# Convolution output and QKV stage joined in one pipeline over batches, Q and K in tiles of 128 rows, attention stacks of batch 0 loaded within it

## The reference, cut to what matters

```
x = x + _L0_conv_ref(_gn(x), ...)          # scan; at its end: layer norm over channels, * ln_weight + ln_bias, gelu
t = _to_tokens(x)
t = t + _L1_attn_ref(_ln_t(t), ...)        # ln, q k v = z @ qkv_w.T + qkv_b, scores + relative bias, softmax, proj
t = t + _L1_ffn_ref(_ln_t(t), ...)
```

## Time and profile before

| what | us |
|---|---|
| median of 3 runs (lowest, highest) | 2886.11 (2885.58, 2888.05) |
| profiled execution, own time | 2886.54 |
| its span | 2884.5 |
| scan, to its last sum | 1398.8 |
| convolution output | 48.7 |
| QKV stage | 131.5 |
| attention up to the first score | 15.2 |

### The profile page before, as it was taken

The page is one execution under the profiler, slowest core; times in us unless marked ns, Lnnn a source line. Parts: engine busy times, 40 slices in busy tenths (PEclk is TensorE's granted clock), DMA queues, the critical chain, the costliest instruction groups (busy, mean ns, idle before and its releaser), DMA issues. The chain is left out here.

```text
span 2884.5 us, 32999 instructions
## 1 busy us (share of the span) xinstructions
PE 2266.9 (79%) x8803; PEld 801.2 (28%) x8803; DVE 2114.8 (73%) x2874; ACT 1339.7 (46%) x1866; POOL 1406.6 (49%) x714
## 2 busy tenths in 40 slices
PE   3676666666666666656576799999999879999999
PEld 1111111111111111111133123322333236766766
DVE  4999999999999999999555788787878652221212
ACT  3445444544454444445455167676767532212121
POOL 3999999999999999999721100000000020000000
PEclk9666757767776766777688599999999979999999
DMA  4544544454455444544314411321312340000000
GB/s 120 173 149 159 179 157 150 161 182 157 140 167 175 164 141 162 173 161 147 117 51 104 54 24 25 42 29 24 46 24 31 61 107 6 6 6 6 6 6 11
DMA packets 97109, 274.03 MB, mean 95 GB/s; under 512 B 16958, under 2 KB 22657, under 8 KB 96897
## 3 DMA queue, kind: packets, MB, share of 16 engines
q1 hardware_dynamic: 92858, 271.89, 33.4%
q10 hardware_dynamic: 4078, 0.19, 0.1%
HBM read 226.55 MB, written 41.22 MB: 93 GB/s over the span
## 5 line engine op out<-in xcount | busy, mean ns | idle before, releaser
L607 POOL TENSOR_TENSOR hs<-hs,c_rep 128x1024 f32<-128x1024 f32 x384 | 897.4, 2355 | 81.1 <-DVE hs L703 51.5
L451 PE MATMUL psU<-b_stack,b_sel 96*128 96x512 bf16 x640 | 310.9, 498 | 451.1 <-DVE hs L703 448.7
L1595 DVE TENSOR_REDUCE mx<-ps 128x1 f32<-128x512 f32 x864 | 539.4, 683 | 115.4 <-PE ps L1434 110.3
L1570 ACT ACTIVATE P<-ps 128x512 f32<-128x512 f32 x768 | 417.7, 599 | 247.1 <-PE ps L1446 223.0
L653 DVE TENSOR_TENSOR psU<-psU,dtu_rep 128x512 f32<-128x512 f32 x640 | 431.3, 679 | 26.8 <-DMA dtu_rep<-dt_rows 10.9
L419 PE MATMUL psY<-hs,state_sel 128*32 128x512 f32 x1572 | 425.9, 904 | 13.8 <-POOL hs L607 8.9
L547 ACT ACTIVATE decay<-dt_rep,a_neg 128x1024 f32<-128x1024 f32 x320 | 360.5, 1140 | 158.4 <-DVE hs L703 134.6
L703 DVE TENSOR_TENSOR_SCAN hs<-decay,hs,psU 128x512 f32<-128x512 f32 x320 | 408.0, 1275 | 2.3
L703 DVE TENSOR_TENSOR_SCAN hs<-decay,psU 128x512 f32<-128x512 f32 x320 | 388.2, 1213 | 0.0
L1434 PE MATMUL ps<-ks,qs 96*128 96x512 bf16 x864 | 344.7, 403 | 34.4 <-DMA ks<-qk_parts 23.8
L451 PEld LDWEIGHTS psU<-b_stack,b_sel 96*128 96x128 bf16 x640 | 62.7, 100 | 975.8 <-DVE hs L703 876.2
(11 more groups left out here) (226 smaller groups left out, 2377.5 us busy)
## 6 DMA issues: line engine op xcount, KB each, us to landing
c_rep<-bc_rows SPq DMA_DIRECT2D x132, 512.0 KB, 4.9
dt_rep<-dt_rows SPq DMA_DIRECT2D x99, 512.0 KB, 4.7
dtu_rep<-dt_rows SPq DMA_DIRECT2D x99, 512.0 KB, 6.3
b_rep<-bc_rows SPq DMA_DIRECT2D x33, 512.0 KB, 6.1
dt_rows<-dt SPq DMA_DIRECT2D x33, 384.0 KB, 3.3
dt_rows<-soft SPq DMA_DIRECT2D x33, 384.0 KB, 3.4
qs<-qk_parts SPq DMA_DIRECT2D x90, 128.0 KB, 6.6
ks<-qk_parts SPq DMA_DIRECT2D x90, 128.0 KB, 7.2
```

The costliest lines, as they stand in the source:

```text
L451: pe.matmul(psU[:, q % UR, :], s.b_sel[:, r, nq, :], b_stack[:, p, CH * pos:CH * pos + CH], start=True, stop=True).then_inc(b_spread, 1)
L607: pool.tensor_tensor(h, h, c_rep[:, nq, :], ALU.mult).then_inc(hc_ready, 1)
L1570: nc.scalar.activation(P[:, kt % 2, head, :], ps2[:, bank, :], ACT.Exp).then_inc(exp_done, 1)
L1595: v.reduce_max(mx[:, slot, u:u + 1], ps1[:, (slot * MAXES + u) % R, :], AX.X).then_inc(max_done, 1)
```

## The change

`conv_out` and `qkv` become one function, `mid`. It runs 24 groups, six a batch: a group is one chunk of 512 tokens and 128 of the 384 rows of Q and K. Both norms are cut into steps, kind 0 for the one ahead of the GELU and kind 1 for the one ahead of Q, K and V. `norm_steps` places them in the groups: kind 0 two batches ahead in groups 0 to 3, kind 1 one batch ahead in groups 3 to 5. GELU of the next batch is run in group 0 (group 1 in batch 0), with a table load before and behind it; x is added in the group after. All norms share a ring of four working buffers in the order of FIRST. The low part is made by POOL (`low_part`), no longer by DVE. The projection's weights and the corner table are prepared before the first group and in group 2, and their copies made in groups 6 and 7. SP loads the stacks of batch 0 in groups 8 to 16, four DMAs each, behind the store of the group. The table's double copy in DRAM is made in `prepare`. V holds 16 columns a head instead of 32, and attention clears and sets its padded copy itself. `layer_norm` stays for the experts' norm.

The core of the diff:

```diff
+Q_PARTS, K_PARTS = [0, 0, 1, 1, 0, 2], [0, 1, 0, 1, 2, 0]
...
+                sp.dma_start(s.ext[0:19, :], w.table).then_inc(tab_ext, 16)
+                sp.dma_start(s.ext[19:37, :], w.table[0:18, :]).then_inc(tab_ext, 16)
+                sp.wait_ge(tab_ext, 32)
...
-def conv_out(nc, w, s):
-def qkv(nc, w, s):
+def mid(nc, w, s):
+        SLOTS, RING, VRING, NORMS = 4, 4, 2, 4
+        MT = 2 * D // 128
+        GROUPS = 2 * MT
+        NQ = GROUPS * NB
+        V_OF = ((0, 1), (2,), (3,), (4, 5), (6,), (7,))
...
+        FIRST = {(0, 0): 0, (0, 1): 1, (1, 0): 2, (1, 1): 3, (0, 2): 4, (0, 3): 5}
+        for b in range(NB - 1):
+            for kind, ahead in ((0, 2), (1, 1)):
+                for c in range(2):
+                    if b + ahead < NB:
+                        FIRST[kind, 2 * (b + ahead) + c] = len(FIRST)
...
+        def norm_steps(b, x, first, second):
+
+            if b == 0 and x < 2:
+                second(0, 2 + x)
+            if b + 2 < NB:
+                if x < 2:
+                    first(0, 2 * (b + 2) + x)
+                if x in (2, 3):
+                    second(0, 2 * (b + 2) + x - 2)
             if b + 1 < NB:
-                (second if x % 2 else first)(2 * (b + 1) + x // 2)
+                if x in (3, 4):
+                    first(1, 2 * (b + 1) + x - 3)
+                if x in (4, 5):
+                    second(1, 2 * (b + 1) + x - 4)
+
+        def gelu_at(b, x):
+
+            return b + 1 < NB and x == (0 if b else 1)
...
+                    at = i - (GROUPS + 2)
+                    if at == 0:
+                        for k in range(SLOTS):
+                            sp.wait_ge(stored[k], 16 * len(range(k, GROUPS, SLOTS)))
+                    if 0 <= at < 9:
+                        for j in (2 * (at % 3), 2 * (at % 3) + 1):
+                            load_stack(at // 3, j)
...
+                def low_part(i):
+                    pool.wait_ge(mid_ready, i + 1)
+                    pool.tensor_tensor(parts[:, i % SLOTS, 2, :], rest[:, i % SLOTS, :], parts[:, i % SLOTS, 1, :],
+                                       ALU.subtract).then_inc(lo_ready, 1)
...
+                for b in range(NB):
+                    for x in range(GROUPS):
+                        i = b * GROUPS + x
+                        if b + 2 < NB:
+                            if x < 2:
+                                add_halves(0, 2 * (b + 2) + x)
+                            if x in (1, 2):
+                                add_squares(0, 2 * (b + 2) + x - 1)
+                        if i:
+                            low_part(i - 1)
+                        if b + 1 < NB:
+                            if x in (4, 5):
+                                add_squares(1, 2 * (b + 1) + x - 4)
+                            if x in (3, 4):
+                                add_halves(1, 2 * (b + 1) + x - 3)
+                low_part(NQ - 1)
...
+                        for j in V_OF[x]:
+                            if nv >= VRING:
+                                pe.wait_ge(v_taken, nv - VRING + 1)
+                            for h in range(2):
+                                t = pe.matmul(ps_v[:, nv % VRING, 0:D], Z[:, b % 2, h, 128 * j:128 * j + 128],
+                                              w_qkv[:, h, 2 * D:3 * D], start=(h == 0), stop=(h == 1))
+                            t.then_inc(v_proj, 1)
+                            nv += 1
+                        norm_steps(b, x, mean, variance)
...
+                def gelu(b):
+                    act.wait_ge(normed, FIRST[0, 2 * b + 1] + 1)
+                    for f in range(2):
+                        nc.scalar.activation(s.Y[:, b, f, :], s.Y[:, b, f, :], ACT.Gelu,
+                                             bias=s.cols[:, COL_LNB + f:COL_LNB + f + 1],
+                                             scale=s.cols[:, COL_LNW + f:COL_LNW + f + 1]).then_inc(gelu_done, 1)
+                    nc.scalar.preload_act_table_set("natural_log_exp_and_others")
...
+                act.wait_ge(own_v, 2)
+                    b, x = i // GROUPS, i % GROUPS
+                    m = x % MT
+                    act.wait_ge(q_proj, i + 1)
+                    nc.scalar.activation(val[:, i % SLOTS, :], ps_w[:, i % RING, :], ACT.Identity,
+                                         bias=qb[:, m:m + 1], scale=scl[:, m:m + 1]).then_inc(q_taken, 1)
+                    act.wait_ge(q_taken, i + 1)
+                        middle_part(i - 1)
+                    norm_steps(b, x, square, invert)
+                    if gelu_at(b, x):
+                        gelu(b + 1)
+                middle_part(NQ - 1)
...
+                add_x(0)
+                centre(1, 0)
+                centre(1, 1)
+                scale(1, 0)
+                centre(0, 2)
+                scale(1, 1)
+                centre(0, 3)
...
+                    v.wait_ge(hi_ready, i + 1)
+                    if i >= SLOTS:
+                        v.wait_ge(lo_ready, i - SLOTS + 1)
+                    v.tensor_tensor(rest[:, i % SLOTS, :], val[:, i % SLOTS, :], parts[:, i % SLOTS, 0, :],
+                                    ALU.subtract).then_inc(rest_ready, 1)
+                    if x and gelu_at(b, x - 1):
+                        add_x(b + 1)
+                    norm_steps(b, x, centre, scale)
+                    if i == 2:
+                        for part in range(QPART):
+                            m = v.tensor_copy(corner_parts[:, :, part, :, :], corners[:])
...
-                for hg in range(NHG):
-                    load(0, hg)
...
-            s.V = sb2("V", [128, NB, 8, HEADS, 32])
-            with nc.sbuf_tensor("Z", [HC, NB, 2, L], F32) as z, nc.sbuf_tensor("raw", [HC, NB, 2, L], F32) as raw:
-                s.Z, s.raw = z, raw
-                conv_out(nc, w, s)
-            with nc.sbuf_tensor("Zq", [HC, NB, 2, L], F32) as z:
-                s.Z = z
-                qkv(nc, w, s)
+            s.V = sb2("V", [128, NB, 8, HEADS, DH])
+            s.qs = sb2("qs", [DH * len(Q_PARTS) + QPART, 3, 4, L], BF16)
+            s.ks = sb2("ks", [DH * len(Q_PARTS) + QPART, 3, 4, L], BF16)
+            s.stack_in = [c2.enter_context(nc.semaphore(f"stack_in{i}")) for i in range(3)]
+            mid(nc, w, s)
```

More of the change, by code:

```diff
@@ L996, in qkv @@
[L996 to L1002, removed]
@@ L1036, in _ @@
-                for i, rows in enumerate((s.first_rows, s.last_rows)):
-                    for part in range(QPART):
-                        sp.dma_start(rows[19 * part:19 * part + 19, :], pick[:, i, :]).then_inc(corner_in, 16)
-                sp.wait_ge(corner_split, 1)
-                for i, stack in enumerate((s.corner_q, s.corner_k)):
-                    for part in range(QPART):
-                        sp.dma_start(stack[19 * part:19 * part + 19, :, :], corner_parts[:, i, part, :, :]).then_inc(corner_in, 16)
@@ L1092, in _, with mean, variance @@
-                for c in range(2):
-                    mean(c)
+                def mean(kind, c):
+                    n = FIRST[kind, c]
+                    pe.wait_ge(both_ready, n + 1)
+                    if n:
+                        pe.wait_ge(centred, n)
+                    pe.matmul(ps_mean[:, :], s.average[:], work[:, n % NORMS, 0, :], start=True, stop=True).then_inc(mean_ready, 1)
+                def variance(kind, c):
+                    n = FIRST[kind, c]
+                    pe.wait_ge(sq_ready, n + 1)
+                    if n:
+                        pe.wait_ge(log_ready, n)
+                    pe.matmul(ps_var[:, :], s.average[:], work[:, n % NORMS, 0, :], start=True, stop=True).then_inc(var_ready, 1)
@@ L1094, in _ @@
+                mean(0, 0)
+                mean(0, 1)
                 pe.wait_ge(w_in, 16)
@@ new lines, in middle_part @@
+                def middle_part(i):
+                    act.wait_ge(rest_ready, i + 1)
+                    nc.scalar.copy(parts[:, i % SLOTS, 1, :], rest[:, i % SLOTS, :]).then_inc(mid_ready, 1)
+                nc.scalar.preload_act_table_set("natural_log_exp_and_others")
+                square(0, 0)
+                square(0, 1)
+                invert(0, 0)
+                invert(0, 1)
+                gelu(0)
+                square(1, 0)
+                square(1, 1)
+                invert(1, 0)
@@ L1160, in _ @@
-                    norm_step(i, square, invert)
-                    act.wait_ge(own_v, 1)
+                    b, x = i // GROUPS, i % GROUPS
+                    m = x % MT
                     if i >= SLOTS:
                         act.wait_ge(rest_ready, i - SLOTS + 1)
-                    for c in range(2):
-                        act.wait_ge(q_proj, 2 * i + c + 1)
-                        nc.scalar.activation(val[:, i % SLOTS, CH * c:CH * c + CH], ps_w[0:HC, (2 * i + c) % RING, :], ACT.Identity,
-                                             bias=qb[:, 2 * qk + f:2 * qk + f + 1], scale=(DH ** -0.5 if qk == 0 else 1.0)
```

(8 more changed lines are left out.)

381 lines of the change are left out of this document (188 added, 193 removed).

## The result

The kernel after takes 2913.69 us (median of 4 runs, 2908.61 to 2914.79) against 2887.08 us before (4 runs, 2885.58 to 2888.48): ratio 1.0089, 95% interval [1.0071, 1.0106]. The forecast was 2897 with a range of 2866 to 2908: the sign is right, the time lies 16.7 us above it and outside the range. The profiled execution took 2913.16 us with a span of 2911.1, 26.6 more than the span before.

The account below looks back on a forecast made before the run. Chains from engine to engine bound the kernel, not full engines, except PE in QKV batches. 39.3 + 50.1 + 49.3 + 41.0 + 23.0 + 3 x 1.1 + 0.2 against 195.4: 10.8 us later, 2897 us, range 2866 to 2908.

Parts of the forecast that it names:

- batch 0: First batch of the pipeline, six groups: 50.1 us, without its collision.
- behind the first score: From the first attention score on: the same in both kernels, so no difference was counted.
- one collision a batch: In batches 0 to 2 DVE's addition of x meets POOL's low part: 1.1 us each; 4.4 us with the start's.
- The loop: Groups 3, 4 and 5 each wait through ACT, POOL, PE and DVE: 8.8, 11.5 and 7.5 us.
- The low part on POOL: Subtraction moved from DVE to POOL: 1.26 us taken, between bounds of 0.68 and 1.26.
- The table loads: ACT's table loads in the stage: 8 expected, 1.28 us each around GELU.
- The clock: PE's granted clock in the first three batches: 0.5 to 0.7.
- rival (a): PE's clock stays high in groups 3 to 5: 11.2 us less, no change, 2886 us; chance 0.24.
- (b): Loops in groups 3 to 5 don't close, POOL or ACT a group ahead: 2826 us if whole; chance 0.19.
- partial form: Only the loops of groups 3 and 5 open: half the gain, some 2860 us; chance 0.14.
- (c): Stores wait behind stack loads and hold ACT's slots in groups 13 to 16: 5 us more, 2902; chance 0.08.
- (d): Each of six table loads on the path costs more than its row: 8 us more, 2905; chance 0.07.

## Why the prediction was wrong

Point by point, the predicted term against the trace (a batch here ends when ACT is free for the next batch's first tile, as in the prediction; collisions included):

| term | predicted | measured |
|---|---|---|
| start of the pipeline | 39.3 | 39.65 |
| batch 0 | 51.2 | 54.4 |
| batch 1 | 50.4 | 51.3 |
| batch 2 | 42.1 | 43.7 |
| from there to attention's block | 23.0 | 22.7 |
| to the first score | 0.2 | 1.0 |
| sum, against 195.4 | 206.2 | 212.7 |
| scan's end | same | 1.6 later |
| behind the first score | same | 7.7 more |

**The step that failed** is the sentence "Everything ahead of the last wave of the scan, and everything behind the first score (64 maxima on DVE, and so on), is the same in both kernels". The prediction had named another time of the attention as a sign of being wrong, but had put no price on it. The instructions are the same; their places in DVE's list are not, and that is worth 6.6 us in the two intervals with the stalls. The test with 13 memsets gave 9.1 us back (7.9 in those two intervals), and with 243 memsets the kernel before got the same long intervals. In the profiled executions the forecast (2897.3) is 15.8 us too low: 7.7 behind the first score, 6.5 in the terms of the stage, and 1.6 from the scan's end, which no edit touches and which lies anywhere between 1394.9 and 1401.7 in the traces of the kernels with the new stage. Without the first of these the kernel would have taken some 2906 us, inside the range. The Trainium skill ("Runtime: NRT & Kernel Launch", section Instruction fetch mechanics) says that instructions are fetched in blocks of 256 and that a taken branch to a block not at hand has to fetch it first. The runs agree with the 256 as far as six places can: of 1222, 1235, 1238, 1246, 1286 and 1478 only the first and the last, 256 apart, have stalls of 4 us or more; the others have 2.3 to 2.8. The intervals hold a second part, the clock behind the stall: 0.70 and 0.72 after the two stalls of the kernel after, 1.00 and 0.74 before, 1.00 and 1.00 with 13 memsets. So of the 7.9 us some 5 are the stalls themselves (9.7 to 4.8). That the clock is most of the rest is an estimate, but one pair shows it apart from the stall: the second intervals of before and of the kernel with 13 memsets have stalls of 2.28 and 2.39 us, clocks of 0.74 and 1.00, and lengths of 52.02 and 50.67.

The DMA records of the two traces show what a long stall has in it that a short one hasn't. Queue 14 carries packets of the kind `instruction`, 8 KB each. In the stall of the kernel after (1858.17 to 1863.25) two of them start, at 1858.83 and 1861.52; in that of before (1838.98 to 1841.33) one, at 1839.38. First after, then before, then the kernel before with 243 memsets over both pieces of its stall (1845.05 to 1849.71):

```profile
q14 instruction: 2, 0.02, 0.8%
...
q14 instruction: 1, 0.01, 1.2%
...
q14 instruction: 2, 0.02, 1.4%
```

With 243 memsets they start at 1845.43 and 1847.85, one ahead of each piece's end. In all traces of this case DVE goes on 1.7 to 2.4 us after the last such packet has started, and every branch back has one packet with the loop at 1235, 1238, 1246 or 1286 and two at 1222 or 1478. The records don't say for which engine a packet is, but the agreement leaves little else than that DVE waits for instructions here, once or twice. Why two packets come one after the other at two of the places, no run here shows.

**A term mis-sized: batch 0, 3.2 us.** In group 3 I had DVE late by the addition of x and the corner table. The group takes 12.3 us where I had 9.9, and group 0 takes 7.55 for 6.4. The timeline of the kernel after has more of group 3:

```profile
1464.55 2.17 DVE L1282 TENSOR_TENSOR Y<-Y,norm_work 96x1024 f32<-96x1024 f32 x1
...
1465.60 2.24 POOL L1081 TENSOR_TENSOR norm_work<-Y 96x512 f32<-96x512 f32 x1
...
1466.64 1.45 DVE L1351 CAST corner_parts<-corners 19x456 bf16<-19x456 f32 x1
...
1471.30 1.21 DVE L1282 TENSOR_TENSOR Y<-Y,norm_work 96x1024 f32<-96x1024 f32 x1
1472.43 1.20 DVE L1274 TENSOR_TENSOR Zq<-Y,ps_mean 96x1024 f32<-96x1024 f32 x1
1473.67 1.06 ACT L1208 ACTIVATE norm_work<-Zq 96x1024 f32<-96x1024 f32 x1 [8.16 <-DVE Zq L1274]
```

Collisions take the scaling to 2.17 us, POOL's addition to 2.24 and a cast of 385 ns to 1.45, and a scaling of the other norm stands ahead of the subtraction, though PE's mean was there at 1469.9 (1467.89 + 2.02). I had counted one collision a batch at 1.1; DVE and POOL meet more often than that. Batches 1 and 2 are off by 0.9 and 1.6 for the same reason, as far as their timelines show.

**Steps that held.** The loop: groups 4 of 11.98, 11.35 and 11.68 us against 11.5, and the low part put last takes 3 us of it away. The low part on POOL: 1187 ns where I took 1.26. The copies of 512 columns: 618 ns for 0.6. The stack loads are hidden. The table loads: eight around the GELUs at 1283 ns, with GELU at 1455.55 right behind one (a ninth, at the stage's start, lies where ACT waits anyway). The clock held less well: 0.72 to 0.77 in the three batches where I wrote 0.5 to 0.7, but 0.53 to 0.71 in groups 3 and 4 and 0.65 to 0.81 in group 5; rival (a) needed it near 1 there. Two numbers of the prediction don't come out of its own rows, and neither changes the forecast: the terms of rival (a) add up to 12.0 us and not 11.2, and a Q/K tile took 1.88 us of PE in the earlier trace rows, not 1.7.

**The rivals.** (a) fell with the clock. (b), loops that don't close, is false of this kernel, but it is what the edits make true: its "partial form" of 2860 stands beside 2858 to 2867 us for the kernels whose squares come a group later. That 2860 was half of a difference and not a sum over groups, so the nearness is in part luck. (c) fell with the loads put back, (d) with the loads' rows.

## What to carry to other kernels

Where an engine serves two chains in program order, put first the operation whose inputs are ready, and behind it the one that waits for the engine it feeds: here two lines were worth 34 us, and turned the change from 0.9% slower to 0.4% faster. Moving work to the idlest engine is no gain if its wait comes along: POOL's low part saved DVE 16 us that were hidden anyway and put a wait of up to 8.8 us ahead of the norm. And when a stage ahead of a loop changes its number of instructions, look at the loop's stalls for "issue" before you believe that the rest of the kernel is unchanged.

## What the runs showed of the hardware that I had not expected

- A loop's branch back on DVE stalls it for 2.3 to 2.8 us or for 4 to 5 us, by its place in the instruction list. Every such stall has one or two 8 KB `instruction` packets in it, and DVE goes on 1.7 to 2.4 us after the last of them starts. The whole effect of 13 instructions was 9.1 us by the medians and 11.6 by the ratios, 0.3 to 0.4% of the kernel.
- Behind a stall of 4 us or more TensorE's granted clock was 0.50 to 0.72 for some 6 us in each case looked at; behind a short one it was 1.00, 0.74 or 0.59. With stalls alike (2.28 and 2.39 us) the interval with 0.74 was 1.35 us longer than the one with 1.00, so a stall of DVE can be paid in part a second time.
- DVE operations with both inputs in SBUF and POOL's additions don't overlap for long, also when each side has only one such operation: an addition of x with one addition of squares took 3.42 instead of 2.43 us for its two halves, and the other 2.03 instead of 1.26; with a low part in between as well, 4.39 and 2.25. The Trainium skill ("GPSIMD Engine Reference", section Specifications) names contention for this pair; the trace adds its size, 0.8 to 2.0 us a meeting.
